# A recommender tower on one core: smaller blocks, resident tables, an order written as one table of steps

## What is computed

```python
combined = jnp.concatenate([dense_features[:, None, :], sparse_features], axis=1)   # [2048, 27, 128]
interactions = jnp.einsum('bfd,bgd->bfg', combined, combined)
iu, ju = jnp.triu_indices(F, k=1)
z = jnp.concatenate([dense_features, interactions[:, iu, ju]], axis=1)
h = jnp.concatenate([z, r_dense_features], axis=1)
h = jnp.maximum(h @ W_top1 + b_top1, 0.0)     # 607 -> 512
h = jnp.maximum(h @ W_top2 + b_top2, 0.0)     # 512 -> 256
y = h @ W_top3                                # 256 -> 1
```

## Time and profile before

| | us |
|---|---|
| median of 3 runs (lowest, highest) | 432.58 (428.92, 434.95) |
| span of the profiled execution | 432.4 |
| PE busy, share of the span | 330.4, 76% |
| POOL busy, share of the span | 308.9, 71% |
| DVE busy, share | 239.1, 55% |
| ACT busy, share | 179.4, 41% |
| mean granted TensorE clock | 0.881 |

### The profile page before, as it was taken

The page is one execution under the profiler, slowest core; times in us unless marked ns, Lnnn a source line. Parts: engine busy times, 40 slices in busy tenths (PEclk is TensorE's granted clock), DMA queues, the critical chain, the costliest instruction groups (busy, mean ns, idle before and its releaser), DMA issues.

```text
span 432.4 us, 13310 instructions
## 1 busy us (share of the span) xinstructions
PE 330.4 (76%) x5360; PEld 266.8 (62%) x5360; DVE 239.1 (55%) x471; ACT 179.4 (41%) x363; POOL 308.9 (71%) x280
## 2 busy tenths in 40 slices
PE   0785719677699998286879999376969999867596
PEld 0563517466578876275668877264758887656475
DVE  2776625397569563266768664075666758023531
ACT  2144223720746546220546545420564546323442
POOL 6887878887778877777778878777777877772000
PEclk9899977888979999659969999666879999986699
DMA  5467853435435345426444543526354442221000
GB/s 155 153 177 191 239 167 109 128 92 151 115 110 149 118 122 117 133 52 167 119 130 114 158 116 106 141 55 169 77 172 100 142 123 71 55 57 28 5 0 0
DMA packets 24707, 49.51 MB, mean 115 GB/s; under 512 B 8010, under 2 KB 10586, under 8 KB 24653
## 3 DMA queue, kind: packets, MB, share of 16 engines
q1 hardware_dynamic: 15916, 30.83, 22.4%
q0 software_dynamic: 8704, 17.84, 17.5%
q10 hardware_dynamic: 32, 0.01, 0.0%
HBM read 48.65 MB, written 0.01 MB: 113 GB/s over the span
## 4 chain that ended last, share of the span: by engine, by line
PE 65%; issue 15%; DMA 10%; ACT 5%; DVE 3%; SPq 0%; ACTq 0%; DVEq 0%
PE mix_ps L454 12%; PE emb_ps L436 12%; PE emb_ps L438 11%; PE emb_ps L416 6%; DMA lookup_ids<-ids_looked_up 5%; DMA table<-table 5%; PE mlp_ps L485 4%; PE mlp_ps L488 4%; PE mlp_ps L486 4%; PE mlp_ps L436 3%; PE mlp_ps L438 3%; DVE one_hot L650 2%; ACT emb L535 2%; PE mlp_ps L498 2%; PE mlp_ps L501 2%
## 5 line engine op out<-in xcount | busy, mean ns | idle before, releaser
L396 POOL DMA_INDIRECT rows<-table,gather_ids x272 | 307.9, 1132 | 83.6 <-issue 81.7
L650 DVE TENSOR_SCALAR one_hot<-lookup_ids,row_number 125x512 fp32r<-125x512 int32 x288 | 124.8, 490 | 43.6 <-DMA lookup_ids<-ids_looked_up 17.6
L436 PE MATMUL emb_ps<-one_hot,table_h 125*128 125x512 f32 x224 | 94.2, 421 | 19.1 <-DVE table_l L640 18.7
L454 PE MATMUL mix_ps<-emb 128*26 128x26 f32 x4096 | 57.7, 202 | 54.3 <-issue 51.5
L438 PE MATMUL emb_ps<-one_hot,table_l 125*128 125x512 f32 x224 | 91.9, 410 | 0.0
L454 PEld LDWEIGHTS mix_ps<-emb 128*26 128x26 f32 x4096 | 49.5, 115 | 63.6 <-issue 61.7
L543 ACT ACTIVATE table_h<-table 125x1024 fp32r<-125x1024 f32 x36 | 38.0, 1060 | 88.9 <-DMA table<-table 52.4
L535 ACT ACTIVATE emb<-emb_ps 128x512 f32<-128x512 f32 (+1 forms) x80 | 46.9, 651 | 56.5 <-PE emb_ps L416 53.2
L663 DVE COPY gram<-mix_ps 128x416 f32<-128x416 f32 x32 | 27.8, 874 | 74.3 <-PE mix_ps L454 74.1
L436 PEld LDWEIGHTS emb_ps<-one_hot,table_h 125*128 125x128 f32 x224 | 44.6, 199 | 31.7 <-ACT emb L535 12.1
L549 ACT ACTIVATE emb<-emb_ps 128x512 f32<-128x512 f32 x28 | 34.0, 1215 | 50.2 <-PE emb_ps L438 50.1
(11 more groups left out here) (50 smaller groups left out, 278.4 us busy)
## 6 DMA issues: line engine op xcount, KB each, us to landing
table<-table SPq DMA_DIRECT2D x36, 500.0 KB
lookup_ids<-ids_looked_up SPq DMA_DIRECT2D x36, 256.0 KB, 5.4
rows<-table,gather_ids POOLq DMA_INDIRECT x272, 3.9
dense_rows<-dense SPq DMA_DIRECT2D x4, 256.0 KB, 4.1
gram<-w_pairs SPq DMA_DIRECT2D x2, 256.0 KB
gram<-w_dense SPq DMA_DIRECT2D x2, 256.0 KB
h_full<-w SPq DMA_DIRECT2D x1, 512.0 KB
gather_ids<-ids_gathered SPq DMA_DIRECT2D x16, 8.5 KB, 10.2
```

The source lines that it names most:

```text
L396: pool.indirect_dma_start(out=rows[:, t, g, :], out_offset=None, in_=tables[GATHERED[g]], in_offset=bass.IndirectOffsetOnAxis(ap=gather_id ...
L436: pe.matmul(bank[:, :], table_h[0:TROWS, i % 2, cols], hot, start=(c == 0), stop=False)
L454: last = pe.matmul(bank[32 * j:32 * j + SIDE, SIDE * q:SIDE * q + SIDE], emb[:, s, 1:FEATURES], emb[:, s, 0:SIDE], start=True, stop=True)
L650: dve.tensor_scalar(one_hot[0:TROWS, hot_slot(i, c), :], lookup_ids[0:TROWS, i % 2, :], row_number[0:TROWS, c:c + 1], None, ALU.is_equal) \
```

## The change

The whole program is rewritten; these are its parts.

- Blocks have 256 samples (8 blocks, 16 tiles of 128). There is no hardware loop: every step of the batch is written out, and all waits are for constants.
- Ten tables (six in the first block) are looked up. Their high and low parts stay in SBUF (`table_hl`), so each is loaded and split once: 10 splits where 36 were. Tables are padded to 1024 rows, indices travel as 16-bit integers, a one-hot matrix has 256 columns, and there are 8 slots for them (9 before). There are 76 lookups of 8 chunks, so 608 one-hot matrices (L571) and 1216 matmuls of 256 columns (L367, L368), where 288 and 576 of 512 columns were.
- 16 tables are gathered (20 in the first block): 264 gathers (L340, 272 before). Their rows go to nine slots of up to four rows each, and POOL waits before each group for the group nine before it to be transposed (`embeds_done`). The dense rows of a tile go into the last slot of the tile.
- Grams come in steps of 16 samples (`BURSTS`), placed between lookup halves. ACT copies them out, two banks; DVE transposes one tile at a time; ACT alone picks the products, in 10 instructions for a tile, for which the pairs have a new order.
- Layers 1 and 2 have matmuls of 256 columns, twice as many; the second writing of the activation stays in PSUM, from where DVE takes the difference (L598). The dense row's parts come straight from PSUM (L579).
- The order of all engines comes from one table of times, in units of a block, that is sorted.

```diff
-LOOKUPS = 9
+FIRST_LOOKUPS, LOOKUPS = 6, 10
+BLOCK = 256
...
+    def look_time(k, h):
+        b, i = LOOKS[k]
+        return b - 1 + (i + h / 2) / (LOOKUPS if b else FIRST_LOOKUPS) + (0.02 if b else 0.0)
...
+    def embed_time(t, e):
+        return (t / 2 - 0.7 if t >= 3 else (-0.2, 0.25, 0.56)[t]) + 0.06 * e * 4 / len(GROUP[t])
...
+                at(t / 2 + 0.05 + 0.24 * (n % 2) + 0.06 * h + (0.07 if t == 1 else 0.0), "gram", n, h)
...
+            for t in range(TILES):
+                if t == 1:
+                    pool.wait_ge(ids_in, 16)
+                for e, group in enumerate(GROUP[t]):
+                    use = GROUP_NO[t, e]
+                    wait(pool, embeds_done, use - ROW_SLOTS + 1)
+                    for q, f in enumerate(group):
+                        if f < FEATURES - 1:
+                            g = f - FIRST_LOOKUPS
+                            pool.indirect_dma_start(
+                                out=rows[:, use % ROW_SLOTS, q, :], out_offset=None, in_=tables[GATHERED[g]],
+                                in_offset=bass.IndirectOffsetOnAxis(ap=gather_ids[:, t, g:g + 1], axis=0),
+                            ).then_inc(rows_in[use % ROW_SLOTS], 16)
...
+                for c in range(h * CHUNKS // 2, (h + 1) * CHUNKS // 2):
+                    n = k * CHUNKS + c
+                    pe.wait_ge(hot_ready, n + 1)
                     cols = slice(DIM * c, DIM * c + DIM)
+                    pe.matmul(bank, table_hl[:, i, 0, cols], hot[:, n % HOTS, :], start=(c == 0), stop=False)
+                    pe.matmul(bank, table_hl[:, i, 1, cols], hot[:, n % HOTS, :],
+                              start=False, stop=(c == CHUNKS - 1)).then_inc(hot_used, 1)
...
+                for q in range(h * HALF // BURSTS, (h + 1) * HALF // BURSTS):
                     for j in range(4):
+                        s = t % 4 * TILE + 32 * j + HALF * side + q
...
+            def split(i):
+                dve.wait_ge(table_high, i + 1)
+                dve.tensor_tensor(table_hl[:, i, 1, :], raw[:, i % RAW, :], table_hl[:, i, 0, :].bitcast(fp32),
+                                  ALU.subtract).then_inc(table_low, 1)
...
+                    dve.tensor_scalar(hot[:, n % HOTS, :], lids[:, k % LIDS, :],
+                                      row_number[:, c:c + 1], None, ALU.is_equal).then_inc(hot_ready, 1)
...
-    nc = bacc.Bacc("TRN2", target_bir_lowering=False, num_devices=1)
+    nc = bacc.Bacc("TRN2", target_bir_lowering=False, num_devices=1, dynamic_dma_scratch_size=4096)
```

More of the change, by code:

```diff
@@ L40, in pair_rows @@
 def pair_rows():
     rows = []
[L43 to L46, removed]
-    return rows
-def dlrm_tower(nc, dense, ids_gathered, ids_looked_up, tables, w1_dense, w1_pairs, b1, w2, b2, w3,
-               out):
+    for r, s in pair_list():
+        a, b = sorted((ORDER[r], ORDER[s + 1]))
+        rows.append(DIM + a * FEATURES - a * (a + 1) // 2 + (b - a - 1))
@@ L64, in dlrm_tower @@
+    GROUP_NO = {use: n for n, use in enumerate(GROUP_USES)}
+    ROW_SLOTS = 9
     CHUNKS = 8
[L65 to L68, removed]
+    HALF, BURSTS = 16, 4
     KCH = [128, 128, PAIRS - 256, DIM]
     N1, N2 = HIDDEN1 // 128, HIDDEN2 // 128
[L71 to L107, removed]
-    EMB_USES = [s for s in TAIL + BODY if s[0] == "embed" or (s in halves and s[2] == 1)]
-    MIX_USES = [("gram", n) for n in range(GRAMS)] + [("z", 0), ("z", 1), ("z", 2)] + [("none",)]
@@ L114, in dlrm_tower @@
-    MLP_USES = [("place", i) for i in range(EARLY)] + [("layer1", n) for n in range(N1)] + \
[L115 to L121, removed]
-    PAIR_ACT = 11
-    first_pair = [r * SIDE - r * (r - 1) // 2 for r in range(SIDE)]
+    HOTS = 8
+    RAW, LIDS = 6, 4
+    LOOKS = [(b, i) for b in range(BLOCKS) for i in range(LOOKUPS if b else FIRST_LOOKUPS)]
@@ new lines, in weights @@
+            def weights(j):
+                act.wait_ge(weights_in, 16 * 9)
+                if j == 3:
+                    act.wait_ge(w1_sum, 1)
+                if j < 4:
+                    act.activation(w1h[:, j, :], w1_stage[:, j, :], ACT.Copy).then_inc(w_high, 1)
+                else:
+                    half = slice(2 * (j - 4), 2 * (j - 4) + 2)
+                    act.activation(w2h[:, half, :], w2_stage[:, half, :], ACT.Copy).then_inc(w_high, 1)
+            run({"split": split, "look": look, "embed": embed, "gram": gram, "pairs": pair_copies, "z": z,
+                 "l1": l1, "l2": l2, "l3": l3, "weights": weights})
```

832 lines of the change are left out of this document (391 added, 441 removed).

## The result

The changed kernel takes 405.4 us (median of 4 runs, 401.8 to 407.2) beside 433.7 for the kernel before (the three runs of its table and a fourth): ratio 0.936, 95% interval 0.929 to 0.944. Forecast were 406 us and a range of 393 to 442. Its profiled execution has a span of 405.4 us.

A forecast was written before the change was run, and what follows sets the result against it. The prediction took PE's list and POOL's gathers as level bounds, PE deciding by a little: 104 us start + 6 blocks x 44 = 368, + 0.5 + 18 + 19.8 = 406 us; 8-in-10 range 393 to 442.

The forecast's parts named there:

- The holes: PE's grams: 51.5 us of waits at instruction packets go, since 6.3 packets a block take 24 us and 16 grams never stand alone.
- PE's list: PE's work for 256 samples: 40.0 us plus 4 of hand-overs, 44.0 us a block (40 to 49.5).
- the weight load: PE's 256-column matmuls: load hidden, 0.122 us each; rival that it shows: 0.160 us each, 464 us in all, chance 0.05.
- hand-overs: PE idle between engines: 4 us a block, at gram copies and one-hots; rival 49.5 us a block, 439 us, chance 0.15.
- The gathers: POOL's gathers: 10 us extra beside subtractions, 16 beside one-hots; last start at 357 us, rows landed at 362.
- gathers and PE level: Main case: POOL's gathers would let the last transpose pass at 362 us, PE at 368; 394 to 423 us, chance 0.62.
- the rival of one-hots on gathers: POOL: one-hots delay gathers by 41 us, giving 425 (chance 0.06), or by 71 us, giving 445 (chance 0.02).
- Start and end: First gram near 37 us, tile 3's rows at 104; after the last transpose 18 us of grams and perceptron, then 19.8.
- my reckoning by packets of 3.8 us: PE behind the last transpose: 1024 + 170 instructions, 4.7 packets of 3.8 us, make 18 us.
- The holes did not stay: Rival at PE's grams: each packet still costs 2 us, 12.6 a block, 482 us; chance 0.03, shared with descriptor space.
- The descriptor space: Rival at POOL: if smaller space held only two gathers, 1.95 us each, time past 500 us; chance 0.03, shared with holes.
- the sign that I had set for being wrong altogether: POOL standing waiting for `embeds_done` would mean PE's list is the bound by an unseen margin.

The follow-up runs named there:

- Run 2: Changed kernel with grams in bursts of 64 samples, one per half tile, in place of 16: 389.3 us, ratio 0.901 to the kernel before.
- run 3: Changed kernel with both 64-sample gram bursts of a tile one behind the other, 512 instructions in a row: 416.5 us, ratio 0.967 to the kernel before.
- run 1: Changed kernel with the MLP's steps 0.06 of a block later in the order of work: 401.4 us, ratio 0.930 to the kernel before.
- run 4: Changed kernel with row numbers for the one-hots 32 bits wide in place of 16: 407.2 us, ratio 0.944 to the kernel before.
- run 6: Kernel before, with only the changed kernel's smaller space for the gathers' descriptors: 432.9 us, ratio 1.004.
- run 5: Changed kernel with nine resident tables in place of ten, the tenth gathered as well: 396.6 us, ratio 0.919 to the kernel before.
- run 12: Changed kernel, 64-sample bursts, eight first-block lookups, seventh block's layer 2 and last product behind the last grams, layer 1 between: 601.6 us, slow chip, ratio 0.866.

## Why the prediction was right, and where its steps were not

**The holes.** "The holes in grams go" holds: 51.5 us became 0.7. The step that laid them to instruction packets holds too: they end 1.2 to 1.8 us behind one. But the reason for their going was half wrong. I argued from the average, 6.3 packets a block spread over 44 us, and from bursts of 16 that never stand alone. Run 2 shows that bursts of 16 are not needed, since bursts of 64 have 3 holes in 32; run 3 shows that a row of 512 brings them back. What matters is the length of the row. That the small bursts cost 16 us against bursts of 64, by their edges and by the later pairs together, was nowhere in the prediction.

**PE's list.** 44.0 forecast, 44.25 measured, by terms that offset each other: luck, as far as the closeness goes. A warm matmul of 256 columns is 0.12 us from start to start, as reckoned (0.122), and the weight load does not show. But 232 of them took 31.6 us, not 28.3: some 0.5 us is the lower clock (run 1), and most of the rest the neighbours of waits and of the 16 bursts, which start 0.2 us apart in place of 0.12. Grams took 5.6, not 6.6. Transposes, of rows and pairs, took 4.6 as against 4.8, layer 3 took 0.56 and not 0.3. The "hand-overs" of 4 us were 1.89: a single wait for pairs, not for gram copies and one-hots, as I had placed them. Run 1 showed the place I named to be the next in line. The clock did not quite stay up, 0.96.

**The gathers.** This is the term furthest off. Forecast 26 us of extra time on 331, with the last start at 357; measured was a last start at 337.7, with gathers of 0.955 us on average, 264 x 0.015 = 4 us above the quiet 0.94, and the two waits for PE, 4.4 us. Both parts were too large. Counted over the rows of after, 180 gathers that meet a one-hot take 0.948 us, 57 that meet neither 0.946, and 27 that meet a subtraction 1.00. The 0.156 us that a one-hot cost before is gone altogether. It is not the 16 bits (run 4) nor the descriptor space (run 6, where gathers stay at 1139 ns); of what remains, the 256 columns are my first guess, but they were not tried by themselves, and neither were the written-out order and the resident tables. The one-hots were busy 190 us, not 172; in a row most of them start 0.26 us apart, near the 0.28 forecast. So "gathers and PE level" was wrong: PE decided alone, with some 20 us of slack under it, which run 5 spent on two more gathers a block, with 16 matmuls of PE fewer, and gained 9 us. Had I weighed the gathers right, the rival of one-hots on gathers (425, 445) would have had next to nothing.

**The shared port.** The changed kernel's rows show one-hots doing nothing to gathers (0.948 against 0.946 us), while the 3.81 us of the earlier trace rows stood beside subtractions. The rule of the Trainium skill (SBUF — State Buffer, section "Who interferes with whom"), by which an instruction of VectorE in a 2-port mode shuts GpSimd out for its whole length, gets no support from them, if these one-hots run in such a mode, which no trace here tells.

**Start and end.** Tile 3's transposes stood at 95.5 us, not 104: that is the gathers' term again, 8 us. The first gram stood at 35.6 (37 forecast). Then 6 blocks of 44.5 to the last transposes at 362.8 (368 forecast). From there to the last gram's end 22.3 us (18.5 forecast: the 2.8 us wait for pairs of tile 13 is in it, and 0.7 of hole, so my reckoning by packets of 3.8 us was the wrong reason, and the value came out too low), then 20.3 (19.8). Sum of the errors: -8.5 at the start, +3.3 in six blocks, +4.3 in the end: -1. That 406 came within 1 us is luck: the start and the end were off by 8.5 and 4.3 us in opposite directions. What the prediction had right is the mechanism of the middle, PE's list of some 44 us a block without holes.

**Rivals.** Hand-overs did not grow (1.89; PE's list is 40.0 of 44.0 us, 91% full and not the 93 that I wrote). The weight load hides: the matmuls of 256 columns start 0.12 us apart. The holes did not stay. The descriptor space costs nothing (run 6). By the sign that I had set for being wrong altogether, GpSimd waiting for `embeds_done`, I was wrong in one step: it waits twice, 4.4 us in all, and PE's list is the bound by a margin that I had not seen, the 20 us of the gathers' term. The time is hardly touched by it, since my sum went by PE's list as well.

## What to carry to other kernels

Count instructions in a row as well as columns: short ones can be used up faster than they are delivered. Here, where the kernel before takes 433 us, other work after 256 of them was enough, and the finest possible mixing was not the best. The shorter pieces cost at their edges and put off whoever waits for the last of them. And where two streams are level, look at which term of each you know least, since an edit that frees one only moves the wait, as run 1 did.

## What the runs showed that I had not expected

- The same program had 18 us of "issue" waits of PE on one chip and 130 us on another, where it took 1.43 times as long; most of the added waits do not end behind an instruction packet, so their cause is probably another than that of the holes; these runs don't tell which. There, too, the five versions with 256-sample blocks that ran stayed ahead of the kernel before (0.845 to 0.866).
- One-hots of 256 columns leave gathers alone (0.948 against 0.946 us), those of 512 columns in the kernel before did not (1.10 against 0.94). The cause is open.
- The 256 grams of a block take more by themselves in bursts of 64 (7.55 us) than in bursts of 16 (5.63), but the neighbours of the short bursts take all of that and 0.6 us more.
- The best version that I found takes 385.7 us, 11% less than the kernel before. It still loses 5.8 us to holes at its end. The version meant to be without them (run 12) ran only on a slow chip, so what it gains is open.
- What each part of the change brings by itself, the resident tables, the smaller blocks, the order without a loop, is not shown: the runs vary the changed kernel's order and its table count, and of the kernel before only the descriptor space.
